# A selective-scan block on one Trainium2 core: stores in blocks between the loads, three projections on half rows, a shorter ffn

## What is computed

```python
xz = x @ W_in;  xh, z = split(xz)                       # x is _ln_c(x); 2 x 512 channels
xc = depthwise_conv3x3(xh)                              # SAME
xp = xc @ W_xproj                                       # 8 + 16 + 16 columns: dt_r, B, C
dt = dt_r @ W_dt + b_dt;  dt_seq = softplus(dt)
dtN = dt_seq @ W_dtN + b_dtN;  A = -exp(A_log)          # 16 states
def step(h, t):                                         # 2304 tokens of an image, in order
    h = exp(dt_t[:, :, None] * A) * h + (dtN_t * B_t)[:, None, :] * x_t[:, :, None]
    y = einsum('bdn,bn->bd', h, C_t) + Dskip * x_t
y = layernorm(y) * ln_g + ln_b;  y = y * silu(z)
x = x + (y @ W_out + b_out)
t = x + ffn(_ln_t(x))
```

## Time and profile before

| | |
|---|---|
| median of 3 runs | 4015.14 us (4010.03 to 4015.31) |
| profiled execution | 4022.24 us, its span 4020.4 us |
| mean granted TensorE clock | 0.854 of 2.4 GHz |
| TensorE busy | 3251.8 us, 81% |
| VectorE busy | 3622.2 us, 90% |
| ScalarE busy | 2944.1 us, 73% |
| GpSimd busy | 3133.2 us, 78% |
| DMA | 790.26 MB, mean 197 GB/s |

### The profile page before, as it was taken

The page is one execution under the profiler, slowest core; times in us unless marked ns, Lnnn a source line. Parts: engine busy times, 40 slices in busy tenths (PEclk is TensorE's granted clock), DMA queues, the critical chain, the costliest instruction groups (busy, mean ns, idle before and its releaser), DMA issues.

```text
span 4020.4 us, 103342 instructions
## 1 busy us (share of the span) xinstructions
PE 3251.8 (81%) x33792; PEld 1589.3 (40%) x33792; DVE 3622.2 (90%) x12317; ACT 2944.1 (73%) x6050; POOL 3133.2 (78%) x5771
## 2 busy tenths in 40 slices
PE   5788888888888888888888888888888888888665
PEld 2334433443344334433443344344433343444333
DVE  2799999999999999999999999999999999999996
ACT  3677777777777787777777777777777777787663
POOL 0788877888888788877888788778877888788874
PEclk7889887889889988988898889888888798889776
DMA  3877878788878787878787878787877888788773
GB/s 67 219 202 203 213 191 206 190 208 205 208 196 214 199 211 196 215 194 205 197 216 199 207 196 213 199 205 193 206 201 199 201 203 209 202 206 205 192 192 80
DMA packets 383392, 790.26 MB, mean 197 GB/s; under 512 B 80517, under 2 KB 235142, under 8 KB 382854
## 3 DMA queue, kind: packets, MB, share of 16 engines
q1 hardware_dynamic: 382854, 783.66, 77.1%
HBM read 648.18 MB, written 96.73 MB: 185 GB/s over the span
## 4 chain that ended last, share of the span: by engine, by line
DVE 31%; PE 31%; ACT 26%; issue 7%; SPq 3%; POOL 2%; DMA 1%; ACTq 0%; POOLq 0%; DVEq 0%
ACT ps_a L638 8%; PE ps_s L583 6%; DVE h L885 6%; PE ps_y L492 6%; PE ps_s L528 4%; DVE ps_a L869 4%; DVE ps_a L872 4%; DVE h L888 4%; PE ps_s L537 3%; ACT ap L648 3%; PE ps_s L566 3%; PE ps_y L476 2%; ACT y L721 2%; DVE sz L941 2%; PE ps_s L584 2%
## 5 line engine op out<-in xcount | busy, mean ns | idle before, releaser
L638 ACT ACTIVATE ps_a<-dtb,a_n 128x384 f32<-128x384 f32 x2304 | 1253.6, 583 | 488.1 <-DVE h L888 472.3
L1169 POOL TENSOR_TENSOR h<-mp,up 128x128 f32<-128x128 f32 x2304 | 1052.5, 457 | 357.6 <-PE ps_y L492 147.4
L1159 POOL TENSOR_TENSOR mp<-ap,h 128x128 f32<-128x128 f32 x2304 | 1051.9, 457 | 358.1 <-ACT ap L648 242.7
L869 DVE TENSOR_TENSOR ps_a<-ps_a,h 128x192 f32<-128x192 f32 x2304 | 813.6, 353 | 239.6 <-ACT ps_a L638 236.7
L885 DVE SCALAR_TENSOR_TENSOR h<-xb,db,ps_a 128x192 f32<-128x192 f32 x2304 | 921.9, 400 | 24.0 <-PE ps_y L492 16.0
L888 DVE SCALAR_TENSOR_TENSOR h<-xb,db,ps_a 128x192 f32<-128x192 f32 x2304 | 927.2, 402 | 0.0
L492 PE MATMUL ps_y<-h,cw 64*32 64x256 f32 x18432 | 787.9, 461 | 71.9 <-DVE h L888 58.0
L872 DVE TENSOR_TENSOR ps_a<-ps_a,h 128x192 f32<-128x192 f32 x2304 | 807.7, 351 | 0.0
L648 ACT ACTIVATE ap<-dtb,a_n 128x256 f32<-128x256 f32 x1152 | 524.2, 509 | 251.1 <-DMA dtb<-xd 233.9
L1149 POOL TENSOR_TENSOR up<-xb,db 128x512 f32<-128x512 f32 x576 | 610.8, 1060 | 3.0 <-DMA xb<-xd 3.0
L492 PEld LDWEIGHTS ps_y<-h,cw 64*32 64x32 f32 x18432 | 315.7, 122 | 488.2 <-DVE h L888 244.6
(11 more groups left out here) (111 smaller groups left out, 4286.5 us busy)
## 6 DMA issues: line engine op xcount, KB each, us to landing
xb<-xd SPq DMA_DIRECT2D x576, 512.0 KB, 7.2
dtb<-xd SPq DMA_DIRECT2D x576, 512.0 KB, 6.3
xs<-xh SPq DMA_DIRECT2D x196, 192.0 KB, 6.2
xd<-dttok SPq DMA_DIRECT2D x288, 128.0 KB, 5.4
xin<-in_x_dram SPq DMA_DIRECT2D x144, 128.0 KB, 6.2
xd<-xtok SPq DMA_DIRECT2D x192, 96.0 KB
res<-in_x_dram SPq DMA_DIRECT2D x144, 128.0 KB, 5.4
out_dram<-res SPq DMA_DIRECT2D x144, 128.0 KB, 3.9
```

Of the source, the lines that this page charges most:

```text
L638: ins = act.activation(ps_a[buf][:, n, 0:2 * VD].rearrange("p (t d) -> p t d", t=2), dtb[:, u % DUNITS, 2 * buf:2 * buf + 2, 0:VD], ACT.Ex ...
L869: dve.tensor_tensor(a[:, 0], a[:, 0], last[:, 0], ALU.mult).then_inc(m0_done, 1)
L1159: pool.tensor_tensor(mp[:, G % 2], ap[:, Q % 2, G % 4], h[:, (G - 1) % HRING, :, VD:HALF], ALU.mult) \
L1169: pool.tensor_tensor(h[:, G % HRING, :, VD:HALF], mp[:, G % 2], up[:, Q % 2, G % 4], ALU.add) \
```

## The change

W_xproj's and W_dtN's outputs are made in two matmuls per group, each over half of the row's 384 tokens, into PSUM partitions 0 to 63 and 64 to 127. xp and the product of B and dtN therefore lie in 128 partitions with half the tokens each. W_dt reads partitions 0 to 8 for one half and 64 to 72 for the other, with the weights twice in SBUF; it takes both shared banks, one per half, for a pair of groups. The stores of x and dt are split by block of 128 tokens and stand in slots 17, 19, 21 and 25, 26, 29; the residual load moves from slot 18 to 13. The bounces become four DMAs. The ffn has 12 stages instead of 14: the compares with 0.5 are folded into the operations that use them, "none set" is handled by masking 16 to 0, and the marks and weights of both nibbles are one operation each.

```diff
-B_ROW, C_ROW, XP_ROWS = 32, 64, 80
+B_ROW, C_ROW, XP_ROWS = 32, 48, 64
+HTOK, HSIDE = TOK // 2, SIDE // 2
...
-    "conv": (0, 1, 3, 4), "xproj": (6,), "dtp": (8, 9, 11, 12), "xtok": (14, 15, 16), "yt": (18, 19, 20, 21),
+    "conv": (0, 1, 3, 4), "xproj": (6,), "dtp": (8, 8, 11, 11), "xtok": (14, 15, 16), "yt": (18, 19, 20, 21),
...
-                for g in range(NG):
-                    load(wdt[0:DTR, g * P:(g + 1) * P].rearrange("r (c p) -> r c p", c=4), dt_cols[g])
...
+                for lo in (0, XP_ROWS):
+                    for g in range(NG):
+                        load(wdt[lo:lo + DTR, g * P:(g + 1) * P].rearrange("r (c p) -> r c p", c=4), dt_cols[g])
...
+                for lo in (B_ROW, XP_ROWS + B_ROW):
+                    load(bdtn[lo:lo + NS, :], b_dtN.rearrange("(n o) -> n o", o=1))
...
-            def store_x(r):
-                sp.wait_ge(xtok_ready, r * KT + KT)
+            def store_x(r, block):
+                sp.wait_ge(xtok_ready, r * KT + block + 1)
...
-                for k, lo, n, j, q0 in X_PARTS:
+                for k, lo, n, j, q0 in X_PARTS[2 * block:2 * block + 2]:
...
-            def store_dt(r):
-                sp.wait_ge(dttok_ready, r * KT + KT)
+            def store_dt(r, k):
+                sp.wait_ge(dttok_ready, r * KT + k + 1)
...
-                for which, src in ((0, dbt[B_ROW:B_ROW + NS]), (1, xp[C_ROW:C_ROW + NS])):
-                    sp.dma_start(bounce[r % 2, which].rearrange("b n w -> n b w"), src).then_inc(bounced, SEM_DMA)
+                for which, src, row in ((0, dbt, B_ROW), (1, xp, C_ROW)):
+                    for half in range(2):
+                        lo = half * XP_ROWS + row
+                        sp.dma_start(bounce[r % 2, which, :, :, half * HSIDE:(half + 1) * HSIDE].rearrange("b n w -> n b w"),
+                                     src[lo:lo + NS]).then_inc(bounced, SEM_DMA)
...
-                    if s == 18 and exists(i - 1):
+                    if s == 13 and exists(i - 1):
                         load_residual(i - 1)
-                    if s == 21 and exists(i + 1):
-                        store_x(i + 1)
-                    if s == 26 and exists(i + 1):
-                        store_dt(i + 1)
+                    if s in (17, 19, 21) and exists(i + 1):
+                        store_x(i + 1, (17, 19, 21).index(s))
+                    if s in (25, 26, 29) and exists(i + 1):
+                        store_dt(i + 1, (25, 26, 29).index(s))
...
-                    mm = pe.matmul(bank[0:XP_ROWS, 0:TOK], wxp[:, g, :], by_step(xc[:, r % 2, g, :]),
-                                   start=g == 0, stop=g == NG - 1)
+                    for half in range(2):
+                        lo = half * XP_ROWS
+                        mm = pe.matmul(bank[lo:lo + XP_ROWS, 0:HTOK], wxp[:, g, :],
+                                       by_step(xc[:, r % 2, g, :])[:, half * QUADS // 2:(half + 1) * QUADS // 2],
+                                       start=g == 0, stop=g == NG - 1, skip_group_check=True)
...
-            def dt_project(r, g):
-                if g == 0:
+            def dt_project(r, pair):
+                if pair == 0:
                     pe.wait_ge(xp_ready, r + 1)
-                bank = take_bank("dtp", r, g)
-                pe.matmul(bank[:, 0:TOK], wdt[:, g * P:(g + 1) * P], xp[0:DTR + 1].rearrange("p b w -> p w b"),
-                          start=True, stop=True).then_inc(dtp_done, 1)
+                banks = [take_bank("dtp", r, 2 * pair + half) for half in range(2)]
+                for n in range(2):
+                    g = 2 * pair + n
+                    for half in range(2):
+                        rows = slice(half * XP_ROWS, half * XP_ROWS + DTR + 1)
+                        mm = pe.matmul(banks[half][:, n * HTOK:(n + 1) * HTOK], wdt[rows, g * P:(g + 1) * P],
+                                       xp[rows].rearrange("p b w -> p w b"), start=n == 0, stop=n == 1,
+                                       skip_group_check=True)
+                        if n == 1:
+                            mm.then_inc(dtp_done, 1)
...
-                               shared_bank("xproj", r, 0)[0:XP_ROWS, 0:TOK].rearrange("p (w b) -> p w b", b=IMAGES),
+                               shared_bank("xproj", r, 0)[:, 0:HTOK].rearrange("p (w b) -> p w b", b=IMAGES),
...
-                act.activation(dt[:, g, :], bank, ACT.Abs).then_inc(sp_abs, 1)
-                act.activation(dttok[:, g * TOK:(g + 1) * TOK], bank, ACT.Relu).then_inc(sp_relu, 1)
+                groups, half = slice(g // 2 * 2, g // 2 * 2 + 2), slice(g % 2 * HTOK, (g % 2 + 1) * HTOK)
+                act.activation(dt[:, groups, half], bank, ACT.Abs).then_inc(sp_abs, 1)
...
+                        if s - 2 in SLOT["dtp"]:
+                            softplus_parts(i + 1, SLOT["dtp"].index(s - 2) + 1)
...
-                    ins = dve.tensor_scalar(hot[:], hot[:], 0.5, None, ALU.is_gt)
+                    for w in range(3):
+                        ins = dve.scalar_tensor_tensor(score[:, :, w, :], hot[:, :, 32 + 8 * w:48 + 8 * w], 0.5,
+                                                       score16[:].unsqueeze(1).broadcast_to([P, KT, 16]),
+                                                       ALU.is_gt, ALU.mult)
...
-                    ins = dve.tensor_scalar(found[:], best[:], 0.0, None, ALU.is_gt)
...
-                    ins = dve.tensor_scalar(best[:], best[:], -1.0, 16.0, ALU.mult, ALU.add)
...
-                    ins = dve.tensor_tensor(nib[:], best[:], found[:], ALU.mult)
...
+                    dve.tensor_scalar(nib[:], best[:], -1.0, 16.0, ALU.mult, ALU.add)
+                    ins = dve.tensor_scalar(amp[:], amp[:], 0.5, 2.0, ALU.is_gt, ALU.mult)
...
+                    dve.tensor_single_scalar(nib[:], nib[:], 15, ALU.bitwise_and)
...
-                for w in range(2):
-                    ins = dve.tensor_tensor(hots[:, :, w, :], rnib[:, :, w:w + 1].broadcast_to([P, KT, 16]),
...
+                ins = dve.tensor_tensor(hots[:], rnib[:].unsqueeze(3).broadcast_to([P, KT, 2, 16]),
...
-                    if 40 <= s < 47:
-                        ffn_stage(i - 1, 2 * (s - 40))
+                    if 41 <= s < 47:
+                        ffn_stage(i - 1, 2 * (s - 41))
```

More of the change, by code:

```diff
@@ L565, in dtn_project @@
                 for g in range(NG):
-                    mm = pe.matmul(bank[0:B_ROW + NS, 0:TOK], wdtn[:, g, :], dt[:, g, :],
-                                   start=g == 0, stop=g == NG - 1)
+                    for half in range(2):
+                        lo = half * XP_ROWS
+                        mm = pe.matmul(bank[lo:lo + XP_ROWS, 0:HTOK], wdtn[:, g, :],
+                                       dt[:, g, half * HTOK:(half + 1) * HTOK],
+                                       start=g == 0, stop=g == NG - 1, skip_group_check=True)
                 mm.then_inc(dtn_done, 1)
@@ L1019, in ffn_weigh @@
                 dve.wait_ge(marked, r * 3 + 1)
-                for w in range(2):
-                    ins = dve.tensor_tensor(hots[:, :, w, :], hots[:, :, w, :],
-                                            amp[:].unsqueeze(2).broadcast_to([P, KT, 16]), ALU.mult)
+                ins = dve.tensor_tensor(hots[:], hots[:], amp[:].unsqueeze(2).unsqueeze(2).broadcast_to([P, KT, 2, 16]),
+                                        ALU.mult)
                 ins.then_inc(marked, 1)
@@ L1203, in _ @@
                                pattern=[[0, 1]], channel_multiplier=1).then_inc(one_set, 1)
+            pool.wait_ge(one_set, 2)
+            pool.affine_select(out=xp_one[:], in_=xp_one[:], compare_op=ALU.not_equal, fill=1.0, base=-(XP_ROWS + DTR),
+                               pattern=[[0, 1]], channel_multiplier=1).then_inc(one_set, 1)
             pool.iota(idx16[:], pattern=[[1, 16]], base=0, channel_multiplier=0,
```

82 lines of the change are left out of this document (38 added, 44 removed).

## The result

The changed kernel takes 4046.44 us (median of 4 runs, 4041.8 to 4052.5); the kernel before took 4015.06 beside it. The ratio is 1.0084, 95% interval 1.0068 to 1.0100. The profiled execution has a span of 4050.7 us, against 4020.4. The forecast was 3853.

What follows compares the result with a forecast made beforehand. VectorE was taken as close to the bound; 1.6 + 1.1 + 0.9 = 3.6 us per row over 46 rows, 166 us, less 4 lost at the start, gave 3860 profiled, 3853 as median. Range 3780 to 3975, the forecast's own 3790 to 3930.

Steps and rivals of the forecast that it cites:

- What bounds the kernel: Whole row: VectorE, busy 90%, is close to the bound, idle 5.6 us per row; TensorE, 81%, is not the bound.
- Stores: SP queue: stores in blocks let the late dtb load land in time; 1.6 us per row, bounds 0 and 2.2.
- rival A: SP queue: loads stay late, store blocks move the lateness to other loads; about 3964 us, chance 0.13.
- The 2.2 us of VectorE's idle time: VectorE's idle 5.6 us per row less the 3.4 of steps 16 and 18, which can hang on the late load.
- Halves: Projections: half-row matmuls run together and shorten the chain to the first softplus part; 1.1 us per row, bounds 0 and 1.9.
- VectorE's waits at steps 16 and 18: Recurrence, waits for ScalarE's decays: to fall from 3.4 to 2.3 us per row as the projections shorten.
- ScalarE's wait for W_dt: Before the first softplus part (L687): 1.71 us in the row shown, to fall under 1.3.
- as now, because both groups of a pair must be in: W_dt to softplus: the first softplus part still comes 1.4 us after W_dt starts.
- Rival B: Projections: the halves don't overlap, 1.1 us less gained per row; 3904 us, chance 0.08.
- Fewer ffn operations: VectorE's ffn: 30 instructions for 33, 12 stages for 14, fewer waits behind GpSimd; 0.9 us per row, bounds 0.2 and 1.9.
- The 0.4 us: VectorE's ffn: gain if, by the skill's rule, the new three-fold compare inherits L978's full wait; 0.4 us instead of 0.9.
- rival D: TensorE: less work leaves its clock low in projections and convolutions; about 4067 us, decides from 0.63 down, chance 0.08.

Runs made afterwards that it cites:

- e16: The kernel before without the bias of W_out (b_out isn't added), nothing else: 3972.32 us, 0.9889.
- e1: The kernel before with only the stores in blocks and the residual load in slot 13: 4008.07 us, 0.9989.
- e5: The kernel before with only the half-row projections, W_dt's two pairs in slots 8 and 12: 3974.84 us, 0.9892.
- e2: The kernel before with only the half-row projections, W_dt's two pairs in slots 8 and 11: 4033.05 us, 1.0057.
- e6: The changed kernel with W_dt's second pair in slot 12 and the 14 ffn stages of before: 3956.52 us, 0.9852.
- e9: The changed kernel with W_dt's second pair in slot 12 and the short ffn's 30 operations over 14 stages, slots 40 to 46: 3922.45 us, 0.9757.
- e7: e4 with the 12 ffn stages in slots 40 to 45 instead of 41 to 46: 3973.65 us, 0.9892.
- e3: The kernel before with only the short ffn, 12 stages in slots 41 to 46: 4033.49 us, 1.0052.
- e4: The changed kernel with W_dt's second pair and its softplus parts one slot later (12 instead of 11): 3978.48 us, 0.9912.
- e8: e3 with the 12 ffn stages in slots 40 to 45: 4040.51 us, 1.0068; its profiled execution took 4016.52 us.
- e17: e9 with W_dt's second pair back in slot 11: 4006.85 us, 0.9961.

## Why the prediction was wrong, step by step

**What bounds the kernel.** It said that VectorE is close to the bound, and that what counts is why it idles. The page itself had another answer in the chain that ended last, which the prediction didn't read. Of the kernel before:

```profile
DVE 31%; PE 31%; ACT 26%; issue 7%; SPq 3%; POOL 2%; DMA 1%; ACTq 0%; POOLq 0%; DVEq 0%
```

TensorE has as large a part of it as VectorE. The row is a ring: TensorE (convolutions to W_dt), ScalarE (softplus to the copy of y), TensorE (W_dtN, W_out and the sums behind it), VectorE (the rest, with ffn). "It is not the bound" was said of TensorE, and e16 puts 45 us on 89 us of it. A high busy share told that VectorE is seldom idle, not that others don't hold it.

**Stores, forecast 1.6 us per row.** The mechanism was right in every row named: ScalarE's wait for dtb under 1 us (2.1 us in all), no block of 12 in the SP queue (8 stores and then 4, 5.58 and 3.02 us; the first two blocks went out as one), and rival A didn't come. The size was wrong: 0.1 us per row alone (0.11% of 4015 over 46 rows), 0.35 with the halves in place. The 2.2 us of VectorE's idle time that hung on the late load were taken for a gain; the chain of e1 shows another path to the same point, ScalarE's copy of y and TensorE's 16.7 us behind it, which was nearly as late. Over all rows VectorE idles 1.58 us per row at step 32 before and 1.50 in e1: ScalarE had released it there, and now TensorE does.

**Halves, forecast 1.1 us per row.** They gave 0.94 us per row (e5), near to the 1.1, but only with the pair in slot 12, and not by the path that was named, so the size was luck. VectorE's waits at steps 16 and 18, 2.7 us per row on average before (3.4 in the row shown), were to fall by 1.1 and are 3.2 in e5; ScalarE's wait for W_dt, to fall under 1.3 us per row, went from 1.7 to 2.0 (82.3 to 94.8 us in all). VectorE's idle time is 398 us in both traces. What fell is its busy time, by 52 us (3622.2 to 3570.6), 24 of them in one 3-element operation (L934, from 1.00 to 0.50 us each) and 10 in `make_db`. The prediction had no such term. As written they cost 0.5 us per row (e2). The step that failed, and that turned the gain into a loss, is the sentence that the first softplus part comes "as now, because both groups of a pair must be in". It looked at the first pair only. The second takes both shared banks in slot 11, and waits there for the second softplus part of the first pair; the change adds a wait, and the prediction didn't name what is queued behind the waiting instruction: the state sums, for which GpSimd waits, then the gates, W_out and the residual. Among the rivals there was none for this. x_project came to 1.52 us (1.4 forecast), W_dtN too; a pair of W_dt came to 2.10 to 2.20 where 1.4 was worked out. Rival B is out for the first two. For W_dt an instruction of 192 columns takes 657 ns against 326 in x_project, and each pair of halves is done in 0.53 us, so the halves overlap, but not in full.

**Fewer ffn operations, forecast 0.9 us per row.** Spread over 14 stages they gave 0.83 us (e6 to e9), near to the forecast; packed into 12 they cost 0.5 us. The prediction counted operations and their holds by GpSimd, and left aside that the recurrence's steps stand between the stages. Two stages fewer put six operations in one place; a hold of 1 us then adds to 2.9 us without a step, and TensorE's sums wait for h. The Trainium skill ("SBUF — State Buffer", "Who interferes with whom") says that a VectorE operation with two SBUF inputs contends with a GpSimd instruction that reads SBUF. The traces agree: L1014, with two such inputs and 0.15 us by itself, starts at 2009.26, just behind GpSimd's input products (L1170, 1.06 us from 2009.21), and lasts 1.02 us; L1019 has a mean of 0.90 in e7. The 0.4 us that the prediction worked out by that rule are nearer than its 0.9, but still a gain where the packed form lost.

**The clock, rival D.** The size was near (4067 said, 4046 measured) and the granted clock too (0.64 in the convolutions, 0.63 the point from which it decides), but that was luck, since the mechanism wasn't the one named. It isn't the less work on TensorE that slows the convolutions: e2, e5 and e9 have the thin projections and convolutions of 400 to 409 us, as before (409.9), and e3 has slow ones with the projections as before. They are slow where TensorE idles for h ahead of them (172 to 192 us of that wait in e3, e4 and the changed kernel, 50 to 74 in e2, e5, e7, e8 and e9). What the low clock costs the whole stays open: from e4 to e7 it only moved, and e8's trace shows an execution without the loss. Of the whole loss the experiments say this: the pair's slot costs 69 us and the packing 49 (e17) or 62 (e9 against e4), the clock's part in the latter included, and against these stand gains of 98 us.

**The sum.** With both slots mended the change gives 98 us (e9) of the 166 forecast: 0.35 + 0.94 + 0.83 = 2.1 us per row and not 3.6. Of the missing 1.5 us, 1.25 are the stores'. The split was wrong too. 2.7 of the 3.6 us were to be idle time of VectorE and 0.9 busy time; from the trace before to that of e9 its busy time fell by 84 us and its idle time by 14. Nor did the range follow from the terms' own bounds: at their lower ends (0, 0 and 0.2 us per row) they come to about 4010 us, above the 3975 at which the range stopped.

## What to carry to other kernels

When two instructions are made one that needs two buffers, look up who frees the later buffer, and list what is queued behind the wait; one slot's difference was worth 1.7% here, four times what the stores gained. Read the chain that ended last beside the busy shares, and test what it says by taking work off that engine: TensorE, busy 81% beside VectorE's 90%, was a bound in its stretch. A wait removed from one path pays only up to the next path that is as late. When a trace is to show that a cause is gone, see that its execution shows the loss, and that the cause didn't move elsewhere. Where a recurrence is interleaved with other operations, their grouping counts like their number: the same 30 operations gained 38 us in 14 stages and lost 24 in 12.

## What the runs showed of the hardware

Two matmuls of 192 columns in different column tiles run together: 16 in 1.52 us, 95 ns each, where the instruction itself lasts 326 ns. Two in different row tiles, with 9 rows of strided input, come to 262 ns each (2.10 us for 8), the instruction lasting 657 ns, and their pace hardly follows the clock: in e6 a pair of W_dt took 2.10 us at a granted clock of 1.00 and the next one 2.20 at 0.50.

A wait of TensorE of some microseconds can be followed by a low clock: idle for 2.53 and 3.98 us ahead of the convolutions, 0.64 and 0.66 granted during them; after gaps of under a microsecond (0.52 us before the change) they ran at 1.00. A gap of 2.98 us that stood before a projection and not before the convolutions (e6) was followed by state sums at 1.96 us instead of 1.09, and then by convolutions at 0.95; one of 2.63 us in the same place before the change left everything at 1.00. So the rows show no fixed rule. When the wait ahead of the convolutions goes, the low clock can turn up behind another one: in e7 the last four matmuls of the input projection, behind 3.26 us of idle time, ran at 0.50. What the low clock costs the whole is not shown by any pair of runs here.
